# A cross-attention and mixture-of-experts kernel: five steps around the first expert tile put in another order

## What is computed

```python
h = _ln(x, ln_g, ln_b)
logits = h @ rw.T + rb
vals, idx = jax.lax.top_k(logits, K)
gates = jax.nn.softmax(vals, axis=-1)
h1 = jax.nn.gelu(jnp.einsum('nd,efd->enf', hf, fc1_w) + fc1_b[:, None, :], approximate=False)
eo = jnp.einsum('enf,edf->end', h1, fc2_w) + fc2_b[:, None, :]
gathered = eo[idx_f, jnp.arange(N)[:, None], :]
mixed = (gathered * gates_f[..., None]).sum(axis=1).reshape(x.shape)
return x + mixed
```

## Time and profile before

| | us |
|---|---|
| median of 3 runs (272.57 to 273.06) | 272.69 |
| the profiled execution | 272.78 |
| its span in the trace | 270.8 |
| TensorE busy | 248.6 (92%) |
| VectorE busy | 184.0 (68%) |
| ScalarE busy | 162.2 (60%) |
| GpSimd busy | 61.6 (23%) |

### The profile page before, as it was taken

The page is one execution under the profiler, slowest core; times in us unless marked ns, Lnnn a source line. Parts: engine busy times, 40 slices in busy tenths (PEclk is TensorE's granted clock), DMA queues, the critical chain, the costliest instruction groups (busy, mean ns, idle before and its releaser), DMA issues.

```text
span 270.8 us, 5195 instructions
## 1 busy us (share of the span) xinstructions
PE 248.6 (92%) x1699; PEld 141.1 (52%) x1699; DVE 184.0 (68%) x369; ACT 162.2 (60%) x289; POOL 61.6 (23%) x110
## 2 busy tenths in 40 slices
PE   6899999999999999899999999998999999999540
PEld 2354533433333433345453455334699999999430
DVE  3859689999989889567554499764377455455543
ACT  3383465676776879869676413871576776766300
POOL 3560000000022020000222020175105700036372
PEclk9999999999999999999999999999999999999955
DMA  7107131240322220530110310013302261122232
GB/s 238 43 9 282 68 90 44 69 113 18 87 65 84 80 80 2 165 114 0 28 61 5 87 32 5 4 50 93 86 19 61 74 189 41 31 59 61 68 87 69
DMA packets 18634, 19.37 MB, mean 72 GB/s; under 512 B 2805, under 2 KB 15025, under 8 KB 18609
## 3 DMA queue, kind: packets, MB, share of 16 engines
q1 hardware_dynamic: 15089, 10.36, 13.2%
q10 hardware_dynamic: 2496, 6.59, 7.6%
q0 software_dynamic: 1024, 2.10, 2.7%
HBM read 9.13 MB, written 5.51 MB: 54 GB/s over the span
## 4 chain that ended last, share of the span: by engine, by line
PE 78%; DVE 9%; issue 3%; POOL 3%; ACT 2%; DMA 2%; POOLq 1%; DVEq 0%; ACTq 0%
PE ps_o L1108 11%; PE ps_r L1184 10%; PE ps_r L1175 10%; PE ps_r L1088 9%; PE ps_o L971 7%; PE ps_r L1046 6%; PE ps_x L946 3%; PE ps_r L982 3%; DVE row_max L808 2%; PE ps_o L1120 2%; PE ps_x L971 2%; PE ps_r L1058 2%; PE ps_o L1115 2%; PE ps_x L975 2%; ACT probs L654 2%
## 5 line engine op out<-in xcount | busy, mean ns | idle before, releaser
L654 ACT ACTIVATE probs<-ps_r 128x1024 f32<-128x1024 f32 (+1 forms) x88 | 83.6, 984 | 26.1 <-PE ps_r L1088 23.2
L804 DVE TENSOR_REDUCE row_max<-ps_r 128x2 f32<-128x1024 f32 x64 | 76.0, 1222 | 13.4 <-PE ps_r L1046 11.9
L704 ACT ACTIVATE parts<-ps_r,staged 128x128 f32<-128x128 f32 x120 | 33.2, 379 | 17.2 <-PE ps_r L1175 16.0
L1108 PE MATMUL ps_o<-probs,v_aug 128*9 128x512 f32 x256 | 33.3, 594 | 0.0
L541 POOL CAST max_part<-row_max 128x16 fp32r<-128x16 f32 x16 | 3.1, 196 | 128.9 <-issue 92.8
L971 PE MATMUL ps_o<-ones_bf 128*128 128x512 bf16 x114 | 32.4, 382 | 0.0
L1175 PE MATMUL ps_r<-rows_T,staged 128*128 128x128 f32 x240 | 30.8, 277 | 0.5 <-DVE staged L893 0.5
L1046 PE MATMUL ps_r<-k_tile,q_tile 32*128 32x512 f32 x128 | 29.9, 480 | 0.9 <-ACT probs L654 0.7
L1184 PE MATMUL ps_r<-staged,parts 128*128 128x128 f32 x240 | 30.7, 275 | 0.0
L1088 PE MATMUL ps_r<-q_tile,k_tile 32*128 32x512 f32 x128 | 29.3, 484 | 1.5 <-ACT probs L654 1.0
L808 DVE TENSOR_REDUCE row_max<-ps_r 128x4 f32<-128x616 f32 x32 | 24.3, 794 | 8.1 <-PE ps_r L1058 7.8
(11 more groups left out here) (161 smaller groups left out, 282.9 us busy)
## 6 DMA issues: line engine op xcount, KB each, us to landing
fc_sb<-fc_w ACTq DMA_DIRECT2D x8, 514.0 KB, 3.6
q_tile<-parts SPq DMA_DIRECT2D x36, 64.0 KB, 2.1
places_in<-o_raw ACTq DMA_DIRECT2D x2, 960.0 KB, 5.2
places_out<-rows_in SPq DMA_DIRECT2D x30, 64.0 KB
rows_in<-places_in SPq DMA_DIRECT2D x6, 256.0 KB, 3.4
k_tile<-parts SPq DMA_DIRECT2D x12, 64.0 KB, 2.1
x_sb<-x SPq DMA_DIRECT2D x2, 256.0 KB, 4.6
fc_sb<-w_rep SPq DMA_DIRECT2D x1, 512.0 KB, 5.3
```

Source lines behind the costliest of these rows:

```text
L654: nc.scalar.activation(probs[:, i:i + w], ps_r[:, slot("s", r), 0:w], ACT.Exp, scale=SCALE).then_inc(s_read, 1)
L704: ins = nc.scalar.activation(hidden[:, n % HIDDEN, c], ps_r[:, slot("s", r), 0, c * P:c * P + P], ACT.Gelu, bias=staged[:, o % STAGES, 2 * ...
L804: nc.vector.tensor_reduce(heads[:, 2 * pair:2 * pair + 2, t], ps_r[:, slot("m", r)], AX.X, ALU.max).then_inc(m_read, 1)
L1108: mm = nc.tensor.matmul(ps_o[32 * j:32 * j + DH + 1, :], v_aug[:, b, c, 4 * g + j], probs[:, region(n) + j], start=first, stop=last, tile_ ...
```

## The change

Three words of the list move. Before, the order is `fc1:0` behind `hT:5`, and `router:1` directly behind it, with `rank:1` ahead of `fc2:0`. After, `fc1:0` stands ahead of `hT:5`, and `fc1:1-2` and `fc2:0` stand ahead of `router:1` and `rank:1`.

```diff
-    warm:3 hT:5 fc1:0 router:1 fc1:1-2 rank:1 fc2:0 xT:1 fc2:1 save:0 fc1:3 stage:4-5 prefix:1 fc1:4-5 scatter:5
+    warm:3 fc1:0 hT:5 fc1:1-2 fc2:0 router:1 rank:1 xT:1 fc2:1 save:0 fc1:3 stage:4-5 prefix:1 fc1:4-5 scatter:5
```

## The result

Beside each other on the same chips the kernel after takes 273.66 us (median of 8 runs, 273.38 to 275.14) and the kernel before 272.66 us (8 runs, 272.24 to 273.06): the ratio is 1.0038, with a 95% interval of 1.0024 to 1.0052. The change makes the kernel 1.0 us slower. 273.65 us was forecast. The profiled execution took 273.78 us, of which 271.8 us are the span.

What follows compares the result with a forecast made beforehand. TensorE, busy without gaps from 209 to 253 us, bounds the kernel, so fc1:4's start decides. Router 1.88 us later less 0.93 off VectorE's chain is 0.95; 272.69 + 0.95 = 273.65 us, range 273.0 to 274.3.

Steps and rivals of the forecast that it cites:

- part 1: TensorE, fc1:0 ahead of hT:5: both through at 194.30 instead of about 195.03, a gain of some 0.7 us.
- part 2: ScalarE, fc1:0 ahead of hT:5: table load right behind rows_T, hT:5 done at 196.03, 1.1 us later, holding nobody.
- Rival C: ScalarE late: table load waits for fc1:0's product, or an equal idle gap follows it; 0.6 us more, 274.25 us; 8%.
- part 3: TensorE, fc1:1-2 and fc2:0 ahead of the router: router starts at 196.97 against 195.09, 1.88 us later.
- part 4: VectorE, copy of fc2:0 ahead of router:1: takes 0.93 us out of the chain, 0.29 copy and 0.64 idle.
- part 5: The sum at fc1:4: 1.88 - 0.93 = 0.95 us later, at 202.74, giving 273.65 us.
- The two new waits: TensorE waits 0.6 us at xT:1 for VectorE to read the logits and 0.5 us at prefix:1 for chosen.
- Rival B: About the same: VectorE's chain behind the ranking shrinks more, as at stage:4; loss 0.5 us, 273.2 us; 12%.
- Rival A: Not slower: TensorE's front gain stays if pick ends by 199.55; fc1:4 0.7 us earlier, 272.0 to 272.7 us; 7%.
- Rival D: The clock: TensorE's waits at xT:1, prefix:1 and fc1:4 drop it to half; 276.5 us or later; 3%.

Runs made afterwards that it cites:

- the first of the two attempts: Kernel before with fc1:0 first, router behind fc1:1, hT:5 ahead of fc1:0's activations on ScalarE, gelu table loaded earlier, five staging buffers: 272.23 us, ratio 0.9983.
- the hole filled: Kernel before with only fc1:0 moved ahead of hT:5, plus seven useless matmuls on TensorE ahead of the router: 273.64 us, ratio 1.0032.
- the second half alone: Kernel before with fc1:1-2 and fc2:0 moved ahead of the router, fc1:0 still behind hT:5: 275.27 us, ratio 1.0100.

## Why the prediction was right
**The front (part 1).** Forecast: `fc1:0` at 192.98, through at 194.30. Measured, with the 0.06 us added: 192.94 and 194.34. Right, as was the remark that this gain is visible and buys nothing.

**ScalarE (part 2).** Forecast: load at 192.85 directly behind `rows_T`, activations behind it, `hT` done at 196.03. Measured: 192.86, 194.15, 195.97. The load didn't wait for the product, and 0.01 us stood between load and activation (194.08 to 194.09 in the rows as they are). The Trainium skill, "ScalarE: Activation LUTs", section "What ACT_TABLE_LOAD costs", has 1.38 us of drain for a switch; this trace shows no such gap, as that of the kernel before didn't. Rival C is out.

**The router (part 3).** 196.97 forecast, 197.02 measured.

**The copy out of the chain (part 4).** Forecast 0.93 us of relief. It is the difference between 1.86 us (logits) and 0.93 us (`fc1:4`: 202.72 - 201.79). The size is right, but the moved copy is only half of it. The run with the copy put back measures the copy: 0.44 us. The other 0.49 us is time that VectorE had stood waiting for `fc2:1` in the kernel before: with 0.44 us for the copy of `fc2:0` it would have been ready for the next at 199.34 + 0.44 = 199.78 and could start at 200.27. That much of a late ranking is swallowed with or without the moved copy, and 1.86 - 0.49 - 0.44 = 0.93. With the copy back, `fc1:4` is 203.24 - 0.08 - 201.79 = 1.37 us later than in the kernel before, which is 1.86 - 0.49.

**The sum (part 5).** 0.95 forecast, 0.93 in the trace, 1.0 in the medians. The two new waits were forecast at 0.6 and 0.5 us and are 0.34 and 0.42; both were covered anyway. The one for `staged` is 1.2 us of 1.1: the sum has 0.5 us from the start of `prefix:1` to the next product, and with the fifth buffer, where nothing else holds `fc1:4`, it is 0.20 us (201.27 to 201.47). For the same reason TensorE by itself would have been at `fc1:4` of the kernel before not at 201.3 but at 201.03 + 0.12 = 201.15, as the run with `stage:4` ahead of `fc2:1` shows. Neither figure enters the 0.95. Rival B wanted the 0.48 us ahead of `stage:4` to shrink; it is 0.48 again (201.91).

**What was right in the number and too narrow in the reason.** The prediction says that `fc1:4` alone decides. Two chains meet there, but VectorE's doesn't end there: with `fc1:4` freed only 0.37 us of the 0.95 came back, and in the kernel before a `fc1:4` that starts 0.64 us earlier brought 0.2 us, which is within the noise. The sentence that VectorE and TensorE are both later, so that their margins stay, is the true one; the shift is VectorE's whole stretch up to about 209 us, and only when that stretch was shortened too did TensorE come back to the times of the kernel before, up to `xT:4`. Rival A has a single condition, at `pick`, and 0.7 us behind it; judging by the first of the two attempts, the slots of `ps_r` would have taken part of that.

**Rival D** was given 3%. In the kernel after it stayed out in the profile. But it came with 0.44 us more of waiting in the profile of one experiment and behind a hole of 1.60 us in that of another, and the times say the same of most of their runs. I had compared with 2.8 us of silence at the end and with a stretch that was busy 2.79 of 4.00 us; neither is a bound for what lies between. 3% was too little.

## What to carry to other kernels
Pulling work forward on the bound engine paid nothing here, because the engine that makes its next weights was behind: ask of each moved word who makes the next buffer or weight, and follow that engine until it first idles, not only to the first meeting point. A chain of small steps that another engine works through (here logits, rank, place) went better ahead of bulk work, in this kernel with and without VectorE relieved. And when a change leaves TensorE waiting in several places close together, the price is the wait and perhaps the clock.

## What the runs showed that I had not expected
- The granted clock fell from 1.00 to 0.50 behind a hole of 1.60 us (`hT:5` to the router; with the hole filled it stayed at 1.00), and behind holes of 0.41 and 1.65 us within 3 us of each other, while holes of 0.34, 0.42 and 1.20 us left it at 1.00 in the profiled execution of the kernel after. The same three with one of 0.73 us ahead of them didn't (the second half alone). The three profiled executions with such a fall took 1.7 to 3.4 us more than was expected of them.
- The last scatter landed after 4.5 us in the execution with the hole filled, where all eight scatters start within 0.02 us of those of the kernel after, and after 4.1 us in another; in the kernel before it took 2.7 us. `load_rows:1` then waits 3.3 to 3.7 us for it, in four of the profiled executions, and 1.3 us in most others. The cause is open.
